# One core, a two-layer decoder: the gate of one stage laid beside the context side of the next, and one engine that collects the ends of the stages

## The reference, cut to what matters

```
xl = alpha[:, None] * value            # end of the layer's first attention
wei = sigmoid(-xl); sw = wei * wei
xo = xl * 2 * sw + 2 * enc * (1 - sw)
x = layernorm(x + xo)

q = (x @ Wq)  ; k = (ctx @ Wk) ; v = (ctx @ Wv)      # 16 heads of 64
scores = q k^T + bias                  # bias [16, 1024, 77], softmax over 77
x = layernorm(x + (softmax(scores) @ v) @ Wo)
```

## Time before, and its profile

| | us |
|---|---|
| median of 3 runs | 2509.54 (2505.22 to 2520.67) |
| profiled execution, its own time | 2514.62 |
| span of its instructions | 2512.8 |
| PE busy | 2299.7 (92%) |
| DVE busy | 1515.9 (60%) |
| ACT busy | 1103.2 (44%) |
| POOL busy | 1078.8 (43%) |
| TensorE clock granted, mean | 0.956 |

### The profile page before, as it was taken

One profiled execution on the slowest core, in us unless ns is written; L12 is line 12 of the kernel. 1 busy time (PEld: TensorE's weight loads), 2 busy tenths in 40 slices (PEclk: granted clock), 3 DMA queues, 4 the chain that ended last, 5 costly groups with the idle time before them and its releaser, 6 DMA issues.

```text
span 2512.8 us, 34569 instructions
## 1 busy us (share of the span) xinstructions
PE 2299.7 (92%) x12918; PEld 1439.0 (57%) x12918; DVE 1515.9 (60%) x2281; ACT 1103.2 (44%) x2349; POOL 1078.8 (43%) x785
## 2 busy tenths in 40 slices
PE   6999999879988999999899998799899589979998
PEld 3333443367754555555555554588566467768887
DVE  6778678447745666773666666432444556656556
ACT  1567567723323444441344444133322457743233
POOL 2456546423443888873578887033401122100000
PEclk7899999999999999999999999899999699989999
DMA  6454333222110111111011111254210141010001
GB/s 124 117 98 89 75 61 78 69 69 48 1 18 1 14 14 14 11 38 31 2 14 15 14 15 14 71 132 133 37 48 23 50 118 51 1 61 16 1 1 34
DMA packets 138067, 114.50 MB, mean 46 GB/s; under 512 B 74823, under 2 KB 115253, under 8 KB 137517
## 3 DMA queue, kind: packets, MB, share of 16 engines
q1 hardware_dynamic: 100749, 111.36, 16.5%
q0 software_dynamic: 36864, 0.15, 4.2%
q10 hardware_dynamic: 288, 0.79, 0.2%
HBM read 86.26 MB, written 13.40 MB: 40 GB/s over the span
## 4 chain that ended last, share of the span: by engine, by line
PE 69%; DVE 11%; DMA 10%; ACT 3%; issue 3%; POOL 2%; SPq 2%; DVEq 0%; POOLq 0%; ACTq 0%
PE PS L120 66%; DMA adj<-e_EE,e_IX 7%; SPq L146 2%; DVE g_SS L124 1%; PE PS L1189 1%; DVE a_MX L733 1%; POOL c_AC L124 1%; ACT a_P L839 1%; DVE c_MX L1790 1%; DVE g_st L1274 1%; DMA a_KS<-a_KL 1%; DVE c_AC L124 1%; DMA a_r<-a_RQ 1%; PE PS L352 1%; POOL adj L345 0%
## 5 line engine op out<-in xcount | busy, mean ns | idle before, releaser
L345 POOL DMA_INDIRECT adj<-e_EE,e_IX x256 | 421.0, 1645 | 463.2 <-DMA adj<-e_EE,e_IX 352.9
L1790 DVE TENSOR_REDUCE c_MX<-PS 128x2 f32<-128x1024 f32 x256 | 313.0, 1223 | 175.7 <-PE PS L120 175.7
L124 POOL TENSOR_TENSOR c_AC<-c_AC,c_P 128x1024 f32<-128x1024 f32 x150 | 381.3, 2542 | 76.9 <-DVE c_AC L124 59.2
L1887 ACT ACTIVATE c_P<-PS 128x1024 f32<-128x1024 f32 x256 | 252.3, 1026 | 225.1 <-PE PS L120 216.9
L733 DVE TENSOR_REDUCE a_MX<-PS 128x2 f32<-128x1024 f32 x256 | 303.5, 1220 | 60.4 <-PE PS L120 59.1
L839 ACT ACTIVATE a_P<-PS 128x512 f32<-128x512 f32 x512 | 270.5, 601 | 88.0 <-PE PS L120 87.1
L120 PE MATMUL PS<-c_P,c_VV 128*64 128x512 f32 x1024 | 249.2, 608 | 0.0
L129 POOL TENSOR_SCALAR e_EQ<-e_KR,e_KC 128x128 bf16<-128x128 f32 x256 | 162.4, 634 | 161.4 <-DMA e_KR<-adj_key 123.9
L120 PE MATMUL PS<-a_QS,a_KS 64*128 64x512 f32 x512 | 194.6, 462 | 19.6 <-ACT a_P L839 8.8
L120 PE MATMUL PS<-a_KS,a_QS 48*128 48x512 f32 x512 | 172.9, 482 | 11.0 <-DMA a_QS<-a_QH 5.7
L120 PEld LDWEIGHTS PS<-a_QS,a_KS 64*128 64x128 f32 x512 | 84.2, 189 | 170.8 <-ACT a_P L839 96.3
(11 more groups left out here) (499 smaller groups left out, 4610.3 us busy)
## 6 DMA issues: line engine op xcount, KB each, us to landing
e_KR<-adj_key SPq DMA_DIRECT2D x64, 256.0 KB, 3.7
f_W<-in_L_ffn_w SPq DMA_DIRECT2D x16, 1024.0 KB, 7.4
c_RB<-c_r SPq DMA_DIRECT2D x60, 128.0 KB, 2.9
g_FB<-in_fside_1x16xSxS SPq DMA_DIRECT2D x8, 616.0 KB, 8.0
a_QS<-a_QH SPq DMA_DIRECT2D x32, 128.0 KB, 4.0
adj<-e_zt SPq DMA_DIRECT2D x16, 256.0 KB, 4.3
adj<-e_EE,e_IX POOLq DMA_INDIRECT x256, 3.2
d_AJ<-adj SPq DMA_DIRECT2D x8, 512.0 KB, 7.3
```

The costliest lines, as they stand in the source:

```text
L124: return v.e.tensor_tensor(o, a, b, op)
L345: g.e.indirect_dma_start(self.adj, bass.IndirectOffsetOnAxis(ap=self.IXE[:, k:k + 1], axis=0), self.EE[:, k:k + 1], None, compute_op=ALU.a ...
L1790: v.e.reduce_max(MX[:, w % 2, :, qt, kh], bank(0, 2).rearrange("p (h n) -> p h n", h=2), AX, negate=True).then_inc(*smax_dve.up())
L1887: s.e.activation(PB[t % NP][:, :, :].rearrange("p h n -> p (h n)"), bank(2 + 2 * (t % 2), 2), ACT.Exp, scale=0.125).then_inc(*st_act.up())
```

## The change

1. **Collector.** `behind` lets SP alone walk the noted ends; SP then raises one semaphore, `begin`, and the other four engines wait for its next value.
2. **Gate inside g.** `stage_gate` becomes a class whose pieces are jobs of stage g's list. With each of the 19 gate steps goes one job of the context side (two at every fourth step). In g, k and wt are now copied by ACT alone; the 16 tiles have one root instead of two.
3. **First scores behind one turned tile.** Tiles 0 to 3 are normalised on ACT; tile 0 is turned, scores 0 follow, and tiles 1 to 3 are turned behind them ("front"). Tiles 4 to 15 are normalised on DVE ("lnorm", two in each of rounds 0 to 5, behind soft) and turned through bank 7 in rounds 1 to 6, two a round, between scores i and out i-2 ("lturn"); ACT copies them ahead of its exponentials.
4. **Places.** g's tiles lie over tiles of stage d that are still held or dead; BM, SS and half of UO lie over EN, so the first BM waits for the gate's last mix.
5. **Stage f.** The load of `L0_ffn_attn_w` is issued behind the four small loads of CR instead of ahead of them.

```diff
     def behind(self, engine):
-        for s, value in self.ends:
-            engine.wait_value(s, value)
+        if not self.stages:
+            return
+        if engine is self.sp:
+            for s, value in self.ends:
+                engine.wait_value(s, value)
+            engine.e.sem_inc(*self.begin.up())
+        else:
+            engine.wait_ge(self.begin, self.stages)
...
+            side = list(context())
+            for n in range(19):
+                yield "gate", n
+                for _ in range(2 if n % 4 == 3 else 1):
+                    if side:
+                        yield side.pop(0)
+            yield "roots",
+            for t in range(4):
+                yield "fnorm", t
+                if t == 1:
+                    yield "front", 0
         for i in range(16 + lag):
             if 2 <= i < 6:
                 yield "u", 1, i - 2
             if i < 16:
                 yield "scores", i
+            for t in range(1, 4) if not (first or i) else ():
+                yield "front", t
...
+                for t in range(2 * i + 2, 2 * i + 4) if 1 <= i < 7 else ():
+                    yield "lturn", t
                 if i < 16:
                     yield "exp", i
                 if 1 <= i < 17:
                     yield "soft", i - 1
+                for t in range(2 * i + 4, 2 * i + 6) if i < 6 else ():
+                    yield "lnorm", t
...
+            elif kind in ("front", "lturn"):
+                t, = a
+                bank_free(7)
+                gate.tensor(t, 7)
+                free[7] = [(gate.xt_act, t + 1)]
...
+                g.wait_ge(gate.mix_dve, 16)
...
-        load("L0_ffn_attn_w", AW[:, :, :], aw_in)
         dma(sp, CR[0:64, :], ...)
...
+        load("L0_ffn_attn_w", AW[:, :, :], aw_in)
```

More of the change, by code:

```diff
@@ L1 @@
+import math
 from contextlib import ExitStack
@@ L992, in load, with stage_ctx @@
             dma(sp, W, A[name].rearrange("(c p) n -> p c n", p=128)).then_inc(*landed.up())
-def stage_ctx(K, block, pre, scale, W, first):
+def stage_ctx(K, block, pre, scale, W, gate=None):
     A, X, XT, CT, bank = K.A, K.X, K.XT, K.CT, K.bank
@@ L1001, in stage_ctx, with sb @@
     E = K.edges
+    first = gate is None
     c = ExitStack()
-    sb = K.sb
+    def sb(c, name, shape, area=None):
+        if first:
+            return K.sb(c, name, shape)
+        area = area or ROOM
+        size = 4 * math.prod(shape[1:])
+        area[1] += -(-size // 32) * 32
+        return K.over(name, area[0], area[1] - -(-size // 32) * 32, shape, F32)
+    FRONT, LATER, ROOM = ["d_WA", 0], ["d_EN", 0], ["d_AJ", 0]
     if first:
@@ L1026, in stage_ctx @@
     udram = K.nc.dram_tensor(pre + "u", [2, 1232, 256], F32, kind="Internal").ap()
+    if not first:
+        gate.signals()
     bo_in, mask_in = K.landing(), K.landing()
@@ L1038, in stage_ctx, with wt_acts, context @@
     lag = 3 if first else 7
-    def schedule():
+    def wt_acts(q):
+        return q // 2 if first else q
+    def context():
         if not first:
@@ L1052, in schedule @@
                 yield "m", k, q
+    def schedule():
+        if first:
+            yield from context()
+        else:
+            side = list(context())
[9 more added lines that the diff above has]
+                    yield "front", 0
         for i in range(16 + lag):
@@ L1171, in tensor @@
                 pe.wait_ge(m_act, 6)
+                if not first:
+                    pe.wait_ge(gate.xt_act, i + 1)
                 for bk, gr in enumerate(groups):
@@ L1198, in tensor @@
                 for j in range(10):
-                    ins = mm(pe, bank(6)[:, 0:256], PT[0:rows[j], i % 2, j, :], UO[0:rows[j], i // 8, j, :], j == 0, j == 9)
+                    ins = mm(pe, bank(6)[:, 0:256], PT[0:rows[j], i % 2, j, :], UO[i // 8][0:rows[j], j, :], j == 0, j == 9)
                 ins.then_inc(*wo_pe.up())
@@ L1232, in vector @@
             bk = place.get(job)
-            if kind == "k":
+            if kind == "k" and first:
                 q, = a
@@ L1237, in vector @@
                 v.e.tensor_copy(KT[:, 3 * q:3 * q + n, :],
-                                bank(bk)[:, 0:154 * n].rearrange("p (a n) -> p a n", n=154)).then_inc(*kp_dve.up())
-            elif kind == "wt" and a[0] % 2 == 0:
+                                bank(bk)[:, 0:154 * n].rearrange("p (a n) -> p a n", n=154)).then_inc(*kp_copy.up())
+            elif kind == "gate":
+                gate.vector(*a)
+            elif kind == "roots":
+                gate.roots_dve()
+            elif kind == "lnorm":
+                gate.norm_dve(*a)
+            elif kind == "wt" and first and a[0] % 2 == 0:
                 q, = a
@@ L1323, in scalar @@
             bk = place.get(job)
-            if kind == "vt":
+            if kind == "gate":
+                gate.scalar(*a)
+            elif kind == "roots":
+                gate.roots_act()
+            elif kind == "fnorm":
+                gate.norm_act(*a)
+            elif kind in ("front", "lturn"):
+                gate.copy_act(*a, 7)
+            elif kind == "vt":
                 q, = a
@@ L1329, in scalar @@
                          bank(bk)[:, 0:154 * n].rearrange("p (a n) -> p a n", n=154)).then_inc(*vp_act.up())
-            elif kind == "wt" and a[0] % 2:
+            elif kind == "k" and not first:
+                q, = a
+                n = len(thirds[q])
+                s.wait_ge(kp_pe, q + 1)
+                s.e.copy(KT[:, 3 * q:3 * q + n, :],
+                         bank(bk)[:, 0:154 * n].rearrange("p (a n) -> p a n", n=154)).then_inc(*kp_copy.up())
+            elif kind == "wt" and (a[0] % 2 or not first):
                 q, = a
@@ L1381, in gpsimd @@
             kind, *a = job
-            if kind == "out" and first:
+            if kind == "gate":
+                gate.gpsimd(*a)
+            elif kind == "out" and first:
                 E.send(g, 3)
```

210 lines of the change are left out of this document (94 added, 116 removed).

## The result

The changed kernel takes 2502.77 us (median of 20 executions, 2493.53 to 2521.5), the kernel before 2512.25 beside it (2498.78 to 2521.96). The ratio is 0.9968 with a 95% interval of 0.9954 to 0.9981: 8 us faster, 5 to 11.5 (the two medians differ by 9.5; from here on a gain by the times is the one by the ratio). A second set of times of the same kernel, taken later, gave 0.9960 (0.9942 to 0.9977). The forecast was 11.0 us.

What follows compares the result with a forecast made beforehand. PE, with 69% of the chain of waits, was taken as the bound, standing still in DVE's gate. Terms -17.4 + 2.0 + 4.4 + 0.0 = -11.0 us gave 2498.5 from the median 2509.5, range 2487 to 2509.

Steps and rivals of the forecast that it cites:

- The begin: Gate's start behind alpha: relay takes 0.3 us, ACT's table load at about 1966.4 instead of 1967.47, 1.0 gained.
- Gate and context: Merged gate and context on DVE: 26.9 gate, 6.5 copies, 4.0 stalls (bounds 1 and 10), ending at 2003.8.
- To scores 0: From DVE's gate end through root, reciprocal, norm, two turns and a copy to scores 0: 2.45 us.
- Scores 0: Two tiles' scores after PE idles: 4.4 us warm plus 1.9 for the slow clock, 6.3.
- S: Last third of scores 0 reaching DVE: forecast at 2012.6 against 2029.98, 17.4 us gained (13 to 20).
- Behind scores 0: Turns of tiles 1 to 3, then ACT's table load: first exponential 4.0 behind S instead of 2.0, 2.0 lost.
- The rounds: Two late turns before out lengthen rounds 2 to 6 by 0.87 us each: 4.4 lost (0 to 7).
- The cover: PE's idle time per round, waiting for DVE's division, taken as 0.31 us to set against 1.18 of late turns.
- Rivals 1 and 3: Late turns and fronts free, PE warm: 2491, chance 0.16; ACT late in rounds, 3.5 a round: 2515, chance 0.08.
- The other ends: Stage ends: into b 0.7 gained, h 0.3 gained, c 1.0 lost, f 0; together 0.0, bounds -2 and +3.
- rival 4: Collector fails, SP walking 2 to 3 us at several ends, or coupled lists end the gate 8 late: 2509, chance 0.10.
- Rival 2: PE stays at 1.2 GHz through gate and context, some 43 us, scores 0 cold: 2507, chance 0.16.

Runs made afterwards that it cites:

- the walks: Changed kernel, but every engine walks its own list of waits at each stage end again: ratio 0.9962 (0.9945 to 0.9979).
- the second profile: The changed kernel itself, unaltered, profiled and timed once more: ratio 0.9960 (0.9942 to 0.9977).
- three places kernel: Against the late pair: POOL's first BM waits for the roots, SP raises the relay before c's fine DMA, attn_w loaded first again; ratio 0.9917.
- the kernel with vt behind: Against the late pair: the three vt stand behind the gate's step 3 instead of between its first steps; ratio 0.9931 (0.9912 to 0.9949).
- the kernel kept warm: Against the late pair: 12 unread matmuls (dummies) on PE between the context's end and the first turn; ratio 0.9948 (0.9925 to 0.9972).
- the late pair: Changed kernel, but a round's two late tiles are turned into one bank and ACT moves both with one copy: ratio 0.9956 (0.9930 to 0.9981).
- the collector alone: The kernel before, with only SP's collector of stage-end waits added: ratio 1.0000 (0.9979 to 1.0021).
- the best kernel: The late pair plus BM behind roots, early relay into c, vt later, separate front banks, six unread PE matmuls: 2488.53 us, ratio 0.9908.

## Why the prediction was right, point by point

**The begin.** 0.3 us for the relay was 0.26. Its gain I had put at 1.0, by ACT's table load; the load is hidden altogether and DVE begins 2.44 us earlier. But, as the walks show, the stall behind it takes a part of this back: 0.6 to 1.9 us of 2.45 are left at the gate's end.

**Gate and context.** The gate's end was forecast at 2003.8, 37.6 us behind alpha, and came at 37.35, and at 35.99 in the second profile. The stop at tile 2 for vt was forecast by the walk through the lists, 4.0 us; it was 5.31 and 3.94. That it comes, where, and for what is the mechanism that bore the prediction, and a walk can give it. That 37.6 lies so near to 37.35 is luck: what is left beside the begin and the stop was 31.8 us in both profiles and had been put at 33.4 (26.9 + 6.5), 1.6 too much, against 1.3 too little for the stop. From alpha to the first exponential it is 50.5 us, for the 50 forecast.

**To scores 0.** 2.45 us were 3.64: the term that was missing is DVE's small operation, 1.01 us for 0.17. The three places kernel shows that POOL makes it, and the rows show how: POOL's first BM runs from 1998.07 for 2.58 us, so to 2000.65, and DVE's operation ends at 2000.67. In the kernel with vt behind, BM starts at 2004.77 and would end at 2007.35; DVE's starts at 2006.91 and takes 0.45, to 2007.36. It waits for POOL's instruction to end, however much of it is left. The reciprocal just before, beside the same BM, took its usual 0.26. The Trainium skill, page "SBUF — State Buffer", section "Who interferes with whom", has it as an exclusive lock on a shared port pair that whoever starts first keeps for its whole instruction, and names DVE instructions with two SBUF inputs among those it holds up; the trace agrees in both cases, and the reciprocal has one input.

**Scores 0.** 6.3 us were 5.85 and 6.83. I had added 1.9 to the warm 4.4 for the slow clock; the kernel kept warm shows the sign and the size (4.41 against 5.83), and from run to run the surcharge is 1.4 to 2.9. It goes with the clock, as the row of the changed kernel from the first matmul of scores 0 to S shows (columns as above):

```profile
2002.66:2008.51 5.85, 5.85 (x14) 3.09 (x14) 1.28 (x2) 0.84 (x2) 0.64 (x1) 0.75 0.00 0
```

5.85 us at a mean granted clock of 0.75, 6.83 at 0.64 in the second profile, 7.30 at 0.60 in the three places kernel and 4.41 at 1.00 in the one kept warm: the product is 4.4 in all four. Together S came 16.98 and 17.36 us earlier, against 17.4.

**Behind scores 0.** The first exponential was to be 4.0 behind S and is 3.70. That is 1.7 lost for the 2.0 forecast, and PE's first turn of probabilities has lost all of it too: it starts 11.10 us behind S, 9.38 before. By scores 2 half of it is back (19.21 and 19.41 us behind S, 18.39 before), and it comes back between that turn and scores 2. Before, then changed:

```profile
2039.37:2048.38 9.01, 9.01 (x31) 5.58 (x32) 1.97 (x4) 5.41 (x27) 0.00 (x0) 0.73 0.30 72
2019.61:2027.72 8.11, 8.11 (x32) 5.15 (x32) 2.56 (x5) 6.58 (x34) 0.00 (x0) 0.81 0.05 15
```

PE is busy throughout in both, with the same work, at a granted clock of 0.73 before and 0.81 now (0.79 in the second profile); time by clock is 6.6 each time. So the 2.0 was nearly right for what it meant, and the sum had nothing for the clock behind it. What is left of the loss at scores 2 is 0.8 to 1.0.

**The rounds.** 0.87 a round were forecast and 0.59 measured, 3.0 for 4.4. The price of a late pair was right (1.18 forecast, 1.12 from 2039.57 to 2040.69 in the chain). The cover was too small: 1.12 - 0.59 = 0.53 lay under idle time of PE, not the 0.31 that the earlier trace rows gives. From the start of out to the start of the turn PE took 4.80 us before and takes 4.32 now (2040.53 to 2044.85): counted from starts, 0.48 of it were idle. Rivals 1 and 3 were each half right, but of other kernels. The late turns can be free (the late pair) and scores 0 can be warm (the dummies). And a late turn can wait behind the exponentials and cost 2.3 us a round; it does so as soon as the order puts it behind out, for bank 7 and not for PE's second turn.

**The other ends.** Into b 0.85 gained (0.7 forecast), into c 0.76 lost (1.0), into h 0.5 gained (0.3), into f nothing (0). The sum of 0.0 was forecast and 0.6 gained was measured. Of rival 4 this much is so: at these ends the collector moves a few tenths both ways.

**Rival 2** falls: the clock is at 0.92 where u, k, wt and m run. A part of m does run at the lower level (6.14 us, 4.47 before), but DVE has no stop above 0.2 us behind tile 2, so the gate does not pay for it; for vt and scores 0 the path does pay. The sum of this rival was also too high: it took u at 4 x 2.7 as twice its warm size, and twice the 3.93 us that the four took before is 7.9, which takes 3 us off its 43.

**What is left.** The stretch gives 13.2 us and the ends 0.6, together 13.8; the two ratios give 8 and 10, with intervals that reach 11.5 and 14.5 (that of the later set takes it in). For the late pair it is 16.2 of the stretch against 11, for the collector alone 2.6 against 0, for the best kernel 24.1 against 23, and for the three places, the other way, 16.2 against 21. Most of the changed kernels come out 1 to 5 us short of their stretch. One profile of the kernel before is the base of all these differences. It is not an outlier: the kernel with the collector alone, with the same gate and g, has 133.58, and with the 2.44 by which its DVE starts earlier that is 136.02. Where the missing microseconds go stays open. The forecast of 11.0 lies between stretch and ratio, and its closeness to the measured 8 to 10 is in part luck: the terms missed by +0.4, -1.2, -1.4 and -0.6 us (S, behind scores 0, rounds, ends), nearly all to one side.

## What to carry to other kernels

Work laid beside other work pays at the seams of the in-order lists: write down for each moved step which list it stands in, what is in front of it there, and whose bank it holds, and walk them; that gave a stop of 4.0 us where 5.3 and 3.9 were measured. Where two small turns share a bank with a copy between them, put both into the bank and copy once: it was worth 3 us here, a quarter of what the whole change gained in its stretch. A faster start is worth less in front of a wait that is there anyway (2.45 us became 0.6 to 1.9 here), so look for the next wait behind a hand-over before giving it a price. And follow a gain to the end of the stretch: 2.1 us won at scores 0 by a warm clock were 0.7 by scores 7.

## What the hardware showed that was not expected

- A DVE operation on 128x4 took 0.17 us alone, 1.01 and 0.45 beside a POOL operation on 128x1232 (2.58 us), always until POOL's had ended.
- SP's walk over waits that were already met took 0.06 us an instruction, twelve of them from 2199.70 to 2200.43.
- The same 12 matmuls of scores 0 reached S in 5.83 to 5.96, 6.77 to 6.83 or 7.24 to 7.30 us behind an idle stretch of PE, and in 4.41 (4.43 in the kernel before) whenever PE had been busy until then. Vt and scores 0 went against each other, and why is not shown: the gate ended at about 36 where DVE's first stall was 4 us and at 37.3 where it was 5.3, and scores 0 took 6.8 to 7.3 in the first case and 5.8 in the second (six profiles that share this order), so that S came within 0.8 us all the same.
